# Another order of the same instructions on the five engines of a Mamba-and-FFN block on one core

## The reference, cut to what matters

```
zxbcdt = u @ W_in.T;  z0, x0 = its first two parts (512 columns each);  xBC, dt = the last 544 + 8
dt = softplus(dt + dt_bias);  A = -exp(A_log);  xBC = silu(causal_conv4(xBC) + conv_b)
h = exp(dt*A)*h + dt * x[...,None]*B;   y = einsum(h, C) + D*x      # a scan over the rows, 8 heads
y = layernorm(y)*ln_gamma + ln_beta;  y = sigmoid(y @ W_gate.T + b_gate) * y
x = x + concatenate([silu(z0) * x0, y]) @ W_out.T
h = gelu(layernorm(x) @ ternary(W_fc).T);  h = layernorm(h)*ln_w + ln_b
x = x + h @ ternary(W_proj).T
```

## Time and profile before

| what | us |
|---|---|
| median of the three runs shown | 1095.89 |
| lowest and highest of them | 1095.04 and 1096.62 |
| the profiled execution, its span | 1095.2 |
| TensorE busy | 1049.7 |
| VectorE, ScalarE, GpSimd busy | 966.7, 962.1, 496.6 |
| table loads on ScalarE: 117 | 150.1 |

### The profile page before, as it was taken

How to read it: one execution, slowest core, us unless ns; L and a number is a source line. 1 busy time by engine, 2 the same in 40 slices (tenths; PEclk the granted TensorE clock), 3 DMA queues, 4 the chain that set the end, 5 groups by cost and what they waited for, 6 DMA issues and landing times.

```text
span 1095.2 us, 23188 instructions
## 1 busy us (share of the span) xinstructions
PE 1049.7 (96%) x8214; PEld 668.4 (61%) x8214; DVE 966.7 (88%) x2007; ACT 962.1 (88%) x1740; POOL 496.6 (45%) x590
## 2 busy tenths in 40 slices
PE   3877999999999999999999999999999999999997
PEld 1543756566575666657565665756666566666674
DVE  5998998999989999988999898899998988788766
ACT  5978698999999988899898999989899997989775
POOL 1543564353534544444434726443263733544552
PEclk9888999999999999999999999999999999999999
DMA  6702434245445265455336564353645433543668
GB/s 199 203 12 39 100 76 78 50 98 116 98 91 95 50 126 98 107 97 96 72 78 116 103 121 87 89 95 62 117 97 113 87 80 63 117 78 64 115 124 161
DMA packets 306708, 105.94 MB, mean 97 GB/s; under 512 B 275488, under 2 KB 302880, under 8 KB 306592
## 3 DMA queue, kind: packets, MB, share of 16 engines
q1 hardware_dynamic: 306592, 104.46, 47.7%
HBM read 24.32 MB, written 8.39 MB: 30 GB/s over the span
## 4 chain that ended last, share of the span: by engine, by line
PE 70%; DVE 11%; ACT 8%; issue 4%; DMA 3%; SPq 2%; POOL 1%; ACTq 0%; DVEq 0%; POOLq 0%
PE bank L399 44%; PE bank L634 8%; PE bank L622 7%; PE bank L560 3%; PE bank L569 2%; PE bank L475 2%; ACT L183 2%; DMA hT<-hb 2%; DVE cv L1018 2%; PE bank L521 1%; DVE EM L1138 1%; DVE st L981 1%; PE bank L545 1%; ACT EM L799 1%; DMA x<-in_x 1%
## 5 line engine op out<-in xcount | busy, mean ns | idle before, releaser
L399 PE MATMUL bank<-xnT,win 128*128 128x512 f16 (+1 forms) x1248 | 299.5, 387 | 19.6 <-DMA xnT<-hb 17.5
L399 PEld LDWEIGHTS bank<-xnT,win 128*128 128x128 f16 (+1 forms) x1248 | 122.2, 102 | 152.3 <-DVE win L930 17.5
L1018 DVE SCALAR_TENSOR_TENSOR cv<-bank,cws,cv 128x510 f32<-128x510 f32 (+5 forms) x240 | 177.4, 745 | 11.1 <-ACT tail L730 3.0
L399 PE MATMUL bank<-yhl,wg 128*128 128x512 f16 x768 | 173.0, 379 | 0.2
L1331 POOL TENSOR_TENSOR caty<-tg,caty 128x512 f16<-128x512 f32 x64 | 83.2, 1309 | 157.8 <-ACT caty L836 157.7
L183 ACT ACT_TABLE_LOAD x117 | 150.1, 1283 | 2.8 <-PEq L1526 0.7
L1326 POOL TENSOR_TENSOR yT<-yhl 128x512 f32<-128x512 f16 x64 | 79.6, 1265 | 113.8 <-DMA yhl<-ynh 113.8
L399 PEld LDWEIGHTS bank<-yhl,wg 128*128 128x128 f16 x768 | 74.3, 98 | 88.3 <-ACT EM L799 1.4
L1335 POOL TENSOR_TENSOR cat<-sz,cat 128x512 f16<-128x512 f32 x64 | 86.2, 1354 | 89.0 <-ACT cat L848 88.6
L634 PE MATMUL bank<-wpj,hT 128*128 128x256 f16 x1024 | 121.2, 273 | 5.2 <-DMA hT<-hb 5.2
L622 PE MATMUL bank<-wfc,x3T 128*128 128x512 f16 x512 | 122.2, 379 | 0.0
(11 more groups left out here) (154 smaller groups left out, 2048.4 us busy)
## 6 DMA issues: line engine op xcount, KB each, us to landing
x<-in_x SPq DMA_DIRECT2D x31, 512.0 KB, 3.8
out_y<-x SPq DMA_DIRECT2D x15, 512.0 KB, 2.9
crep<-cv SPq DMA_DIRECT2D x128, 32.0 KB, 2.0
hT<-hb SPq DMA_TRANSPOSE x128, 3.2
caty<-in_wg SPq DMA_DIRECT2D x1, 1024.0 KB, 7.2
x<-in_wout SPq DMA_DIRECT2D x1, 1024.0 KB, 6.7
hT<-in_wfc SPq DMA_DIRECT2D x1, 1024.0 KB, 6.1
hb<-in_wpj SPq DMA_DIRECT2D x1, 1024.0 KB, 8.4
```

What stands on the lines that cost most here:

```text
L399: m = eng.matmul(b, lhs(p, k), rhs(q, k), start=(n == 0), stop=(n == len(seq) - 1))
L1018: op = eng.scalar_tensor_tensor(cs[0:w, j, 3 - k:T], b[0:w, 0:T - 3 + k], cws[0:w, j, k:k + 1], cs[0:w, j, 3 - k:T], ALU.mult, ALU.add)
```

## The change: what it does

Only the five strings differ. Every step is there as often as before, with the same instructions on the same data, and the waits are made from the steps. TensorE's words also name other banks. The number of table loads that ScalarE's order asks for goes from 117 to 122. The lines of the diff that are told of below, a line or two of each table:

```
 PE_ORDER = (
-    "c00 c01 c02 u03 v04 c05 c06 B07 z00 c13 m01 x02 x05 c10 x06 c14 z07 v02 u11 c15 g03701 x06 z03 s07 b00 c11 "
-    "q034 q027 O05 e06 v03 t04 z00 v02 q075 r06340 w0 w0 q075 c21 w0 m17 w0 c25 y06 y03 u24 y07 z10 s12 x14 z16 "
...
+    "c00 c01 u02 c03 c04 B05 c06 z07 v00 c12 c11 m03 x04 c17 x06 x00 u15 c12 x03 z05 v04 g06035 s01 b06 e00 O03 "
+    "z05 q074 v05 c11 q020 v03 t07 z04 q065 r02074 w0 w0 q065 c21 w0 w0 m16 z15 y02 y00 c27 y03 u26 s14 x15 q121 "
...
 SP_ORDER = (
-    "h0 h0 h0 h0 W0 K0 K0 h1 h1 W0 c0 W0 W0 60 h2 h2 c1 61 n0 n0 n0 n0 c2 W0 h3 h3 62 r0 n1 n1 n1 n1 r1 c3 X0 X0 "
...
+    "W0 h0 h0 h0 h0 K0 W0 W0 K0 h1 h1 c0 W0 60 h2 h2 61 n0 c1 n0 W0 n0 n0 h3 c2 h3 62 r0 n1 n1 n1 n1 c3 X0 X0 h4 "
```

## The result

The changed kernel takes 1113.22 us in the median of four runs (1111.19 to 1113.91), the kernel before 1095.99 (four runs, 1095.04 to 1096.62). The ratio is 1.0151, with an interval of 1.0137 to 1.0165, so the change costs 15.0 to 18.1 us. I had forecast 1105, with a range of 1097 to 1112: the direction was right, the size was not, and the median lies 1.2 us outside the range.

The account below looks back on a forecast made before the run. TensorE was taken to pace 150 to 1050 us, VectorE the start and a last chain the end. Terms 10.5 + 0 + 0 - 3 + 0.4 + 1.3 = +9.2 us gave 1104.4, forecast as 1105 us, range 1097 to 1112.

Parts of the forecast that it names:

- TensorE is the pace of the 900 us: From 150 to 1050 us TensorE has only 4.47 us idle, so each microsecond it loses there costs the program one.
- TensorE is not the pace: Rival, chance 0.14: VectorE and ScalarE pace the 900 us, the 10.5 us vanish in existing waits; 1094.6 us.
- Narrow steps, +10.5: On TensorE, q steps in 62 places instead of 41 and more narrow-mode entries and exits cost 10.5 us (6 to 12.5).
- TensorE's waits, 0: TensorE's 4.47 us of idle time in the 900 us could vanish or grow; taken as 0 (-4.5 to +8).
- VectorE near the start, -3: Moving line 1116 later in blocks 0 and 1 fills three VectorE waits, so TensorE's full stretch starts earlier: -3 us (-10 to 0).
- SP +0.4: At the start, loading gate weights W0 ahead of the four transposing DMAs delays the first product: +0.4 us (0 to +2.3).
- the end +1.3: One more projection step ahead of the last block's line 622 matmuls delays gelu and the last chain: +1.3 us (0 to +2).
- ScalarE's five loads, 0: Five more table loads, 6.4 us, lie in ScalarE's 79 us free in the 900 us; taken as 0.
- New waits: Rival, chance 0.16: finer order leaves ScalarE hand-overs uncovered; 6.4 us of table loads plus 2 to 3 us waits, 1114 us.

Follow-up runs that it names:

- the kernel whose pairs had to share banks: Order of after; on TensorE alone all 30 separated pairs of q steps put side by side again, 17 places sharing a bank: 1134.19 us, ratio 1.0358 to before.

## Why the prediction missed its size

**TensorE is the pace of the 900 us: right.** It stays at 99.4%, and taking pairs apart on this engine alone costs its full price (6.1 us in mode changes, 9.2 in all). "TensorE is not the pace" is out.

**Narrow steps, +10.5: right, a little small.** The traces show +11.4 for the 900 us (12.1 with the other choice of prices), where I had 9.5 + 1. The prices read from two places in the earlier trace rows held in every kernel: 0.096 us for an entry into a q step, 0.105 for its exit to a wide step.

**TensorE's waits, 0: too low by 1 to 2.4 us.** After itself has 0.9 more than before, the mean of its middle 2.4. I had reasoned that the added 10.5 us leave the other engines more time. But of the 13 waits of TensorE that the profile of after lists in the 900 us, 12 are for ScalarE or VectorE. That it is the distance of the steps that counts, and not the time per block, is my reading and not shown. Why after's middle waits more is seen only as small gaps of up to 0.9 us; I can't say which of its moves makes each.

**VectorE near the start, -3: the step that failed.** "With all three waits gone VectorE is 3.75 us earlier when block 1 ends its scan." The waits went and the scan ended at 122.07 instead of 122.7. Filling them in before's order alone gave +1.4 us (-0.1 to +2.8), and the whole start of after costs 2.0. Two things were wrong in it. The longest of the waits came with the half clock in some executions and is not the order's. And the step took VectorE's waits for time on the path of the scan, while new waits for ScalarE came in their place (1.22 and 2.04 us in after, 1.15 where VectorE's order alone was changed). In that last trace the scan of block 1 ended at 121.8, 0.9 us earlier than in before's, where the step had reckoned 3.75. That is an error of 4 to 5 us, the largest of the sum. Which move of the start costs the 2.0 stays open. The work that fills the 2.48 us takes about 7 us in the trace of the changed VectorE, not 8, which changes nothing.

**SP +0.4 and the end +1.3: neither contradicted nor shown** (+0.2 with -1.3 to +1.8, and +1.0 with -0.5 to +2.5). The distance from gelu to the end grew by 0.5 us.

**ScalarE's five loads, 0:** not tested by themselves. They can't have cost TensorE more than the 2.4 us by which its waits in the middle grew, so not the 6.4 of the rival. "New waits" gave 1114 us and came nearest to the result, but mostly by luck: it added 6.4 us of loads, where the 7.3 us that the forecast lacked are for the most part the start.

With what the traces showed for the middle and the comparisons for start and end, the sum is 11.4 + 2.4 + 2.0 + 1.0 = 16.8 us; measured are 16.5 (15.0 to 18.1). The closeness is in part luck: the terms of start and end are uncertain by 1.5 us each, and by comparisons alone the sum is 19.

## What to carry to other kernels

Read a change of order on a full engine from start-to-start distances by kind of neighbour, and count the kinds: this term came out within about a tenth, though busy time hides it. Before a wait near the start is booked as a gain, see whether it is there in a second execution and whether the clock was low beside it; fill a wait only if what stands behind the filled work is not on the same chain. And a pair of narrow steps is cheap only while the banks for both are free together: the kernel whose pairs had to share banks was slower than the one with single steps.

## What was not expected of the hardware

One order of the start ran in two ways in six executions. In three the clock was at 0.89, 0.83 to 0.89, 0.89 in the three windows and the scan of block 1 ended at 122.6 to 123.3 us; in the other three it was at 1.00, 0.85, 0.97 to 0.98 and ended at 118.8 to 119.0, some 4 us earlier. Such a difference is half of the spread of before's runs, 1092.51 to 1100.29 us in 29 of them. The time of a run goes with its mean granted clock there: the five runs at 0.994 and 0.995 took 1093.2 to 1094.8 us, the four at 0.989 took 1098.0 to 1100.3. The prices of the mode changes, on the other hand, are the same in every trace: a step o followed by a q step has a median of 0.096 us above its usual distance in all twelve traces.
